# An attention and expert kernel: early Q/K parts moved to ScalarE and GpSimd, five banks in the last unit, routing reordered

## The chip, the cores and the metric

One core of one Trainium2 chip runs the whole program. The metric is device time in microseconds; the kernel before took 1055.47 us (median of 3 runs, 1055.44 to 1056.58). Engines are named as in the profile: PE (TensorE, with its weight loads as PEld), DVE (VectorE), ACT (ScalarE), POOL (GpSimd), SP (SyncE, which issues most DMAs).

## The reference, cut to what matters

Cross-attention of 4 batches of 512 image tokens on 1601 context rows (16 heads of 16), with a small MLP behind it, and then a layer with one shared expert and 8 routed experts of which each token takes two.

```python
def _L0_xattn_ref(x, y, Wq, bq, Wk, bk, Wv, bv, W1, b1, W2, b2):
    q = (x @ Wq + bq).reshape(B, N, NUM_HEADS, HEAD_DIM)
    k = (y @ Wk + bk).reshape(B, M, NUM_HEADS, HEAD_DIM)
    v = (y @ Wv + bv).reshape(B, M, NUM_HEADS, HEAD_DIM)
    scores = jnp.einsum('bnhd,bmhd->bhnm', q, k) * scale
    attn = jax.nn.softmax(scores, axis=-1)
    out = jnp.einsum('bhnm,bmhd->bnhd', attn, v).reshape(B, N, IMAGE_DIM)
    h = jax.nn.relu(out @ W1 + b1)
    return h @ W2 + b2
...
probs = jax.nn.sigmoid(logits)
scores, idx = jax.lax.top_k(probs, TOP_K)
cw = (jax.nn.one_hot(idx, E_ROUTED, dtype=x.dtype) * scores[..., None]).sum(-2)
out = shared
for e in range(E_ROUTED):
    out = out + cw[..., e:e + 1] * _expert(x, Wg[e], Wu[e], Wd[e])
...
x = x + jnp.tanh(g_xattn[0]) * _L0_xattn_ref(_layernorm(x, axis=-1), ctx_768, ...)
x = x + jnp.tanh(g_ffn[0]) * _L0_ffn_ref(_layernorm(x, axis=-1), ...)
```

## The kernel before, in words

Attention runs in 16 units: 4 batches times 4 groups of four heads. Q and K of a batch are made in two halves of 128 rows (dt 0 and 1): 2 jobs ("Q", b, dt) and 8 jobs ("K", b, dt, q), each a product in a bank of `ring_ps`. ACT adds the bias and writes the value rounded to fp32r, the high part (L643, L648); DVE subtracts that from the product again and so writes the low part (L1017, L1024). SP then copies high and low rows into the stacks `kst` and `qst` of a unit by DMA (L448, L452, L467, L469): a unit multiplies stacks of high and low rows.

Every unit has two passes over its scores. First the maxima: 26 "pairs" ("S", u, ...) are two matmuls of 512 keys into one of two slots of `gu_ps` (L839), each reduced by DVE (L985, or L987 for the last 68 keys, 1.2 us and 0.7 us); then ("MX", u) turns the 16 maxima (L779), DVE negates them into `mneg` (L1032), and SP writes them as one more row of `qst` (L474). Second the values: 13 steps of four transposed score tiles `st` (L852, one for each head, in banks of `ring_ps`), four exponentials on ACT (L690), and four products with V into `pv_ps` (`pv`, L867). Between the tiles of a step stand the other jobs: the pairs of the next unit, V, the sums ("SUM"), the MLP of the batch before, and in the last unit the transposes and logits of the second layer ("XT2", "LT", "LG").

Four things set the order. `schedule()` writes it out by hand: `first` and `early` before the first step, then for each step a `chunk` of pairs and a list of jobs; unit 1's first six pairs stand ahead of the first step, the other 20 go into unit 0's steps. `ring` gives each user of `ring_ps` a bank in turn, three banks in all, and PE waits until the user three places before has been emptied (`free_bank`). `probs` has two buffers: the first exponential of a step waits until the `pv` two steps back is done. And each engine has one queue in program order.

The second layer (`experts`) runs as 16 shared tiles and 39 blocks of routed tokens on one pipeline, i = 0 to 56: in step i PE makes gate and up of tile i (`gate_up`, L1359), turns the hidden tile i-1 (`turn_hidden`, L1368) and multiplies tile i-2 down (`down`, L1379), which DVE takes out (`take_y`, L1556 or L1561). The first 10 shared tiles cover the routing. In step 2 DVE does `route()` (L1445 to L1462) from the logits, for which ACT does one exponential (L1268) and loads its table; in step 3 PE counts (`ranks`) and DVE computes slots; in steps 4 and 5 DVE and ACT build one-hot rows (`make_hot`, `make_rows`); in step 6 PE inverts them (`inverse`, L1316) and DVE makes the lists (`make_lists`). DVE also splits the experts' weights into high and low parts in these steps (`rest_gate` L1542, `rest_up` L1547, 16 calls), and the first routed block waits for all of them. Weights arrive by DMA meanwhile.

Of the kernel before, what the change touches and what calls it, by code (L numbers as in the profile page):

```python
# [62 lines left out]
AT_REST = {5: range(0, 3), 6: range(3, 8)}  # L63
# [4 lines left out]
LEAD = 3  # L68
NR = 3
NSP = 2  # L70
# [43 lines left out]
def schedule():  # L114
# [61 lines left out]
    parts = [k[6:7], k[7:8], q[1:2]] + [[("V", 0, g, i)] for g in range(VJOBS) for i in range(min(2, MT - 2 * g))]  # L176
# [5 lines left out]
    for n, pair in enumerate(ahead):  # L182
        early += [pair] + (parts.pop(0) if parts else [])
    b = B - 1
# [114 lines left out]
def attention(nc, I, x1, stats, mv, veps, power, rstd, tg, ident, rows_dram,  # L299
# [11 lines left out]

    ring = list(before)
    for u, mt, _, jobs in steps:
        m = MT * u + mt
        mids, tops = [job for job in jobs if job[0] != "MX"], [job for job in jobs if job[0] == "MX"]
        ring += [("st", idx) for idx in (4 * m - 1, 4 * m) if idx >= 0] + mids
        ring += [("st", 4 * m + 1), ("st", 4 * m + 2)] + tops
    ring += [("st", 4 * MT * UNITS - 1)] + last_jobs
    ring_at = {user: n for n, user in enumerate(ring)}

    def bank(user):

        return ring_at[user] % NR

    def bank_owner(user):

        n = ring_at[user]
        return ring[n - NR] if n >= NR else None

    by_act = [job for job in order if job[0] in ("XT", "V", "OT", "W1")]  # L330
    by_dve = [job for job in order if job[0] not in ("XT", "V", "OT", "W1")]
# [8 lines left out]
    with ExitStack() as ctx:  # L340
# [10 lines left out]


# [44 lines left out]
        hi_ready = sem("hi_ready")  # L397
        xn_ready = sem("xn_ready")
# [23 lines left out]
        def _(sp):  # L422
# [19 lines left out]
            def load_first_stacks():  # L442
# [3 lines left out]
                sp.wait_ge(free_dve, freed["K", 0, 0, 1])  # L446
                for c, part in ((0, 0), (1, 1), (2, 0)):
                    sp.dma_start(kst[0][c:P:4, :, half].bitcast(F32), kc[0:64, 0, part, half].bitcast(F32)  # L448
                                 ).then_inc(half_loaded, 16)
                sp.wait_ge(free_dve, freed["Q", 0, 0])  # L450
                for c, part in ((0, 0), (1, 0), (2, 1)):
# [1203 lines left out]
```

## Time and profile before

| | |
|---|---|
| median of 3 runs | 1055.47 us |
| the profiled execution's own time | 1053.79 us |
| its span, first to last instruction | 1052.0 us |
| mean granted PE clock | 0.995 |
| PE / DVE / ACT / POOL busy | 1020.6 / 675.8 / 610.3 / 204.0 us |
| start to the first step of unit 0 | 0 to 63.8 us |
| units 0 to 14, steps | 63.8 to 684 us |
| last unit, steps | 684 to 728 us |
| end of attention and MLP | 728 to 749 us |
| shared tiles with the routing | 749 to 810 us |
| routed blocks and the end | 810 to 1052 us |

A busy PE is not PE at its peak, because matmuls overlap and their ends are modelled; where PE waits is read from the timeline and the chain of waits. The span's own start is 0 in all times below.

### The profile page before, as it was taken

The page shows a single profiled execution, that of the slowest core. Times are in us where ns is not written, and L with a number is a line of the kernel's source. Part 1 is how long each engine was busy: PE and PEld are TensorE (multiplying, and loading weights), DVE is VectorE, ACT ScalarE, POOL GpSimd, SP SyncE. Part 2 cuts the span into 40 slices and gives each one's busy share as a digit, 9 for nine tenths or more (in the row PEclk, how much of TensorE's full clock was granted, in tenths as well). Part 3 has the DMA queues.
Part 4 walks back from the last instruction along what each step waited for, and adds up shares of the span by engine and source line. Part 5 has one row for each costly group of instructions (what it writes and reads, how often), then busy time and mean ns, then how long its engine had stood idle before and what let it go on. Part 6 is the DMA issues. An engine that isn't in the chain of part 4 may idle for free. (4 is left out here: it accounts for less than half of the span.)

```text
span 1052.0 us, 15631 instructions
## 1 busy us (share of the span) xinstructions
PE 1020.6 (97%) x5729; PEld 548.4 (52%) x5729; DVE 675.8 (64%) x920; ACT 610.3 (58%) x1139; POOL 204.0 (19%) x212
## 2 busy tenths in 40 slices
PE   5889999999999999999999999999989999999998
PEld 3443445343545434444444353333656888888865
DVE  4989787896677798578788678621388333222226
ACT  2148777887577777577787667774356222222221
POOL 5018400008200003600000031020003233333310
PEclk9989999999999999999999999999999999999999
DMA  8361130430303313113033020110491011111207
GB/s 199 88 165 26 38 64 1 126 63 1 62 2 62 91 36 62 41 23 63 1 63 63 1 62 2 36 55 32 159 342 31 31 51 51 50 52 55 50 26 239
DMA packets 38281, 70.15 MB, mean 67 GB/s; under 512 B 6848, under 2 KB 23360, under 8 KB 38208
## 3 DMA queue, kind: packets, MB, share of 16 engines
q1 hardware_dynamic: 33072, 57.88, 21.2%
q0 software_dynamic: 3744, 10.23, 3.2%
q10 hardware_dynamic: 1392, 1.05, 0.4%
q8 instruction: 48, 0.79, 0.3%
q14 instruction: 25, 0.20, 0.1%
HBM read 33.70 MB, written 9.31 MB: 41 GB/s over the span
## 5 line engine op out<-in xcount | busy, mean ns | idle before, releaser
L690 ACT ACTIVATE probs<-ring_ps 128x512 f32<-128x512 f32 (+1 forms) x832 | 441.6, 598 | 136.3 <-PE ring_ps L852 132.9
L985 DVE TENSOR_REDUCE mpart<-gu_ps 128x2 f32<-128x1024 f32 x384 | 457.0, 1221 | 82.6 <-PE gu_ps L839 82.6
L852 PE MATMUL ring_ps<-qst,kst 64*128 64x512 f32 (+1 forms) x832 | 232.1, 464 | 3.7 <-ACT probs L690 3.1
L867 PE MATMUL pv_ps<-probs,vp 128*32 128x512 f32 (+2 forms) x1664 | 222.1, 606 | 0.7 <-ACT probs L690 0.7
L852 PEld LDWEIGHTS ring_ps<-qst,kst 64*128 64x128 f32 (+1 forms) x832 | 100.9, 181 | 218.6 <-ACT probs L690 125.1
L839 PE MATMUL gu_ps<-kst,qst 63*128 63x512 f32 (+1 forms) x1024 | 178.4, 397 | 8.4 <-DVE mpart L985 7.0
L839 PEld LDWEIGHTS gu_ps<-kst,qst 63*128 63x128 f32 x1024 | 92.2, 186 | 68.4 <-DVE mpart L985 43.5
L1205 ACT ACTIVATE h_sb<-gu_ps 128x512 f32<-128x512 f32 x55 | 32.8, 596 | 135.8 <-PE gu_ps L1359 135.7
L1412 DVE TENSOR_TENSOR h_sb<-h_sb,gu_ps 128x512 f32<-128x512 f32 x55 | 37.8, 687 | 112.6 <-ACT h_sb L1205 112.1
L294 POOL TENSOR_SCALAR veps<-mv 128x4 f32<-128x4 f32 x8 | 1.9, 232 | 533.8 <-DVE mv L954 283.6
L1379 PE MATMUL y_ps<-wd,hT 128*128 x312 | 73.8, 379 | 0.0
L1196 POOL DMA_INDIRECT picked<-ysb,target x39 | 38.5, 988 | 131.7 <-DVE ysb L1561 131.7
L867 PEld LDWEIGHTS pv_ps<-probs,vp 128*32 128x32 f32 (+2 forms) x1664 | 32.4, 107 | 57.3 <-issue 42.9
L1359 PE MATMUL gu_ps<-wgu_lo,xb_hi 128*128 x156 | 61.2, 392 | 0.0
L1379 PEld LDWEIGHTS y_ps<-wd,hT 128*128 128x128 f32 x312 | 56.2, 190 | 6.0
L1359 PE MATMUL gu_ps<-cold,parts 128*128 128x512 f32 x118 | 53.6, 595 | 0.3 <-PEq L340 0.3
L1183 POOL DMA_INDIRECT xb<-rows,token x39 | 40.7, 1044 | 60.8 <-DVE token L1517 39.0
L1211 ACT ACTIVATE xb_hi<-t_ps 128x256 fp32r<-128x256 f32 x39 | 15.0, 385 | 49.3 <-PE t_ps L1325 49.3
L1561 DVE COPY ysb<-y_ps 128x256 f32<-128x256 f32 x39 | 16.6, 425 | 33.1 <-PE y_ps L1379 33.1
L662 ACT ACTIVATE vp<-ring_ps 128x512 f32<-128x512 f32 (+1 forms) x28 | 15.9, 568 | 34.1 <-PE ring_ps L727 34.1
L1246 ACT ACTIVATE hT<-ht_ps 128x512 f32<-128x512 f32 x55 | 32.5, 592 | 3.6 <-PE ht_ps L1368 3.6
L1024 DVE SCALAR_TENSOR_TENSOR parts<-ring_ps,bk,parts 128x402 fp32r<-128x402 f32 (+1 forms) x32 | 20.3, 635 | 22.2 <-ACT parts L648 22.1
(205 smaller groups left out, 1146.6 us busy)
## 6 DMA issues: line engine op xcount, KB each, us to landing
kst<-parts SPq DMA_DIRECT2D x45, 401.0 KB, 5.3
qst<-parts SPq DMA_DIRECT2D x48, 128.0 KB, 4.5
wgu<-in_WgT SPq DMA_DIRECT2D x16, 256.0 KB, 8.5
wgu<-in_WuT SPq DMA_DIRECT2D x16, 256.0 KB, 8.6
wd<-in_WdT SPq DMA_DIRECT2D x8, 512.0 KB, 9.7
wgu<-picked SPq DMA_DIRECT2D x8, 512.0 KB, 8.5
cold<-in_ctxT SPq DMA_DIRECT2D x3, 800.5 KB, 4.1
cold<-in_ctxT SPq DMA_DIRECT2D x6, 400.2 KB, 5.9
```

The lines of the kernel that those rows point to most:

```text
L690: nc.scalar.activation(probs[0:w, m % NPB, h, :], ring_ps[0:w, bank(("st", idx)), :], ACT.Exp, scale=SCALE).then_inc(exp_done, 1)
L839: last = nc.tensor.matmul(out, qst[u % NKB][rows, p, i * P:(i + 1) * P], kst[u % NKB][rows, p, keys], start=True, stop=True)
L852: nc.tensor.matmul(ring_ps[0:w, bank(("st", idx)), :], kst[u % NKB][rows, h // 2, mt * P:mt * P + w], qst[u % NKB][rows, h // 2, :], start ...
L867: last = nc.tensor.matmul(pv_ps[32 * h:32 * h + c1 - c0, :], values[:, c0:c1], probs[0:w, m % NPB, h, :], start=(mt == 0), stop=(mt == MT ...
L985: nc.vector.tensor_reduce(mpart[:, :, p, t, q], s_ps[:, n % NSP], AX.X, ALU.max).then_inc(s_free, 1)
L1183: pool.indirect_dma_start(xb[:, r % NXB, :], None, rows_dram[:], bass.IndirectOffsetOnAxis(ap=token[:, r:r + 1], axis=0)).then_inc(xb_load ...
L1196: pool.indirect_dma_start(picked_dram[:], bass.IndirectOffsetOnAxis(ap=target[:, r:r + 1], axis=0), ysb[:, r % NXB, :], None).then_inc(y_s ...
L1205: nc.scalar.activation(h_sb[:, i % 2, :], gu_ps[:, i % 2, 0, :], ACT.Silu).then_inc(silu_done, 1)
L1246: nc.scalar.activation(hT[:, i % 2].rearrange("p k n -> p (k n)"), ht_ps[:, i % 2, :], ACT.Copy).then_inc(ht_copied, 1)
L1359: last = nc.tensor.matmul(gu_ps[:, i % 2, f, :], x, w, start=(n == 0 and not begun), stop=(n == len(products) - 1))
L1379: last = nc.tensor.matmul(y_of(i), hT[:, i % 2, k, :], w, start=(k == 0), stop=(k == FK - 1))
L1412: nc.vector.tensor_tensor(h_sb[:, i % 2, :], h_sb[:, i % 2, :], gu_ps[:, i % 2, 1, :], ALU.mult).then_inc(h_ready, 1)
```

## The change

Five things are changed.

1. Start. PE does 48 transposes of the identity before its first real product. The stack copies of the first unit are issued as soon as the part that each needs is written, the high parts before the low ones. The second half (dt 1) of batch 0's Q and K is emptied by ACT alone: a second activation writes the unrounded value, and POOL subtracts the high part in place.
2. Unit 0. Of unit 1's pairs two stand ahead of the first step and 24 go into the ten steps up to its maxima, so three in some steps; the last V job goes into step 0.
3. Last unit. Ring users take five banks in turn, the two further ones in `gu_ps`, whose slot 1 no pair needs any more; the tiles of each step run two tiles further ahead, and all jobs stand behind the four tiles and ahead of `pv`.
4. The wait for all pairs ahead of the shared tiles goes; a wait for all exponentials stands ahead of the last product of the attention part.
5. Routing. ACT's exponential comes ahead of the copy of tile 1's hidden rows; DVE takes out tile 0 inside `route()`, behind the maxima; the first three `rest_gate` move from step 5 into step 6, ahead of the lists.

PE, start of the program; `L770` and `L822` are K, `L748` and `L800` the transposes of x, `L755` and `L807` Q, `L839` and `L891` the pairs, before:

```order
L770 MATMUL ring_ps<-cold,w_kv 128x402 x2
L748 MATMUL ring_ps<-ident,xn 128x128 x8
L770 MATMUL ring_ps<-cold,w_kv 128x402 x2
L755 MATMUL ring_ps<-xnT,wq 128x512 x2
L770 MATMUL ring_ps<-cold,w_kv 128x400 x4
L770 MATMUL ring_ps<-cold,w_kv 128x402 x4
L839 MATMUL gu_ps<-kst,qst 128x512 x4
```

and now:

```order
L927 MATMUL ring_ps<-ident 128x128 x48
L822 MATMUL ring_ps<-cold,w_kv 128x402 x2
L800 MATMUL ring_ps<-ident,xn 128x128 x8
L822 MATMUL ring_ps<-cold,w_kv 128x402 x2
L807 MATMUL ring_ps<-xnT,wq 128x512 x2
L822 MATMUL ring_ps<-cold,w_kv 128x400 x4
L822 MATMUL ring_ps<-cold,w_kv 128x402 x4
L891 MATMUL gu_ps<-kst,qst 128x512 x4
```

Only the 48 transposes are new there; the order behind them stands.

PE in two steps of the last unit (`L852`, `L906` the tiles; `L867`, `L921` pv; `L795`, `L847` XT2; `L801`, `L853` LT), before:

```order
L852 MATMUL ring_ps<-qst0,kst0 128x512 x2
L795 MATMUL ring_ps<-ident,parts 128x128 x4
L852 MATMUL ring_ps<-qst0,kst0 128x512 x2
L867 MATMUL pv_ps<-probs,vp 32x512 x3
L867 MATMUL pv_ps<-probs,vp 17x512
L852 MATMUL ring_ps<-qst0,kst0 128x512 x2
L801 MATMUL ring_ps<-parts,wr 8x512 x2
L852 MATMUL ring_ps<-qst0,kst0 128x512 x2
L867 MATMUL pv_ps<-probs,vp 32x512 x3
L867 MATMUL pv_ps<-probs,vp 17x512
```

and now, where `gu_ps` rows are those in the two further banks:

```order
L906 MATMUL gu_ps<-qst0,kst0 128x512
L906 MATMUL ring_ps<-qst0,kst0 128x512 x3
L847 MATMUL gu_ps<-ident,parts 128x128 x4
L921 MATMUL pv_ps<-probs,vp 32x512 x3
L921 MATMUL pv_ps<-probs,vp 17x512
L906 MATMUL gu_ps<-qst0,kst0 128x512
L906 MATMUL ring_ps<-qst0,kst0 128x512 x3
L853 MATMUL gu_ps<-parts,wr 8x512 x2
L921 MATMUL pv_ps<-probs,vp 32x512 x3
L921 MATMUL pv_ps<-probs,vp 17x512
```

The job has moved from between the tiles to behind them, next to `pv`.

DVE in the routing (`L1556`, `L1504` take_y; `L1412`, `L1468` the hidden tile), before:

```order
L1452 MAX top<-prob 128x8 x16
L1455 MAX_INDEX top_i<-top,prob 128x8 x16
L1457 CAST top_f<-top_i 128x128
L1459 TENSOR_TENSOR hot<-count_f,top_f 128x128 x2
L1462 TENSOR_TENSOR cnt<-hot 128x128
L1556 SCALAR_TENSOR_TENSOR x<-y_ps,tg,x 128x256
L1412 TENSOR_TENSOR h_sb<-h_sb,gu_ps 128x512
```

and now:

```order
L1521 MAX top<-prob 128x8 x16
L1504 SCALAR_TENSOR_TENSOR x<-y_ps,tg,x 128x256
L1525 MAX_INDEX top_i<-top,prob 128x8 x16
L1527 CAST top_f<-top_i 128x128
L1529 TENSOR_TENSOR hot<-count_f,top_f 128x128 x2
L1532 TENSOR_TENSOR cnt<-hot 128x128
L1468 TENSOR_TENSOR h_sb<-h_sb,gu_ps 128x512
```

Tile 0 is taken out four rows of DVE work earlier, and the counts are written one row of work later.

The diff, cut to its core:

```diff
-AT_REST = {5: range(0, 3), 6: range(3, 8)}
+AT_REST = {6: range(3, 8)}
+BEGUN = 2
+WARM = 48
 NR = 3
+NX = 2
...
         for n, chunk in enumerate(scores(u)):
             at = start + n * MT // len(scores(u))
+            if u == 1:
+                at = (n - BEGUN) * (MT - LEAD) // (len(scores(u)) - BEGUN)
...
+    others[0].append(("V", 0, VJOBS - 1))
...
+    def ahead_of_values(u, job):
+        return job[0] == "MX" or u == UNITS - 1
+
+    def tiles_of(m):
+        first, last = (2 if m > MT * (UNITS - 1) else 0), (2 if m >= MT * (UNITS - 1) else 0)
+        return list(range(max(4 * m - 1 + first, 0), min(4 * m + 3 + last, 4 * MT * UNITS)))
...
+    widened = ring_at["st", 4 * MT * (UNITS - 1)]
+    narrowed = ring_at[last_jobs[0]]
+    for n, user in enumerate(ring):
+        count_of = NR + NX if widened <= n < narrowed else NR
+        turn = (turn + 1) % count_of if n else 0
+        banks[user], owners[user] = turn, held.get(turn)
+        held[turn] = user
...
+    by_pool = [job for job in order if job[0] in ("Q", "K") and job[1:3] == (0, 1)]
+    by_act = [job for job in order if job[0] in ("XT", "V", "OT", "W1") or job in by_pool]
...
-                sp.wait_ge(free_dve, freed["K", 0, 0, 1])
-                for c, part in ((0, 0), (1, 1), (2, 0)):
...
+                for part, copies, done, at in ((0, (0, 2), hi_ready, hi_count["K", 0, 0, 1]),
+                                               (1, (1,), free_dve, freed["K", 0, 0, 1])):
+                    sp.wait_ge(done, at)
+                    for c in copies:
+                        sp.dma_start(kst[0][c:P:4, :, half].bitcast(F32), kc[0:64, 0, part, half].bitcast(F32)
+                                     ).then_inc(half_loaded, 16)
...
+                if b == 0 and hg // 2 == 1:
+                    sp.wait_ge(low_ready, len(by_pool))
...
+            for job in by_pool:
+                dt, cols = job[2], slice(KCUT[job[3]], KCUT[job[3] + 1]) if job[0] == "K" else slice(0, N)
+                part = kc if job[0] == "K" else qc
+                pool.wait_ge(free_act, freed[job])
+                nc.gpsimd.tensor_tensor(part[:, dt, 1, cols], part[:, dt, 1, cols].bitcast(F32),
+                                        part[:, dt, 0, cols].bitcast(F32), ALU.subtract).then_inc(low_ready, 1)
...
+                    if job in by_pool:
+                        nc.scalar.activation(qc[:, dt, 1, :].bitcast(F32), slot, ACT.Identity, bias=bq[:, dt:dt + 1]
+                                             ).then_inc(free_act, 1)
...
             pe.wait_ge(pool_ready, 2)
+            for n in range(WARM):
+                nc.tensor.transpose(ring_ps[:, 0, 0:P], ident[:], ident[:])
...
-            pe.wait_ge(free_act, freed["V", 0, VJOBS - 1])
...
-            pe.wait_ge(s_free, len(pairs))
...
+            pe.wait_ge(exp_done, 4 * MT * UNITS)
             begin_shared(1, 0, 0)
...
                 if i < JOBS:
                     silu(i)
+                if i == AT_LOGITS:
+                    act.wait_ge(logits_ready, 1)
+                    nc.scalar.activation(prob[:], logit[:], ACT.Exp, scale=-1.0).then_inc(exp_ready, 1)
                 if i >= 1:
                     take_ht(i - 1)
...
                 for t in range(TT):
                     last = nc.vector.max(top[:, t, :], prob[:, t, :])
                 own(last)
+                take_y(0)
...
                 if i == AT_INVERSE:
+                    for e in range(3):
+                        rest_gate(e)
                     make_lists()
...
-                if i >= 2:
+                if i > 2:
                     take_y(i - 2)
```

## Rows read from the trace of the kernel before

**Rows 1.** The page, busy time and share of the span.

```profile
PE 1020.6 (97%) x5729; PEld 548.4 (52%) x5729; DVE 675.8 (64%) x920; ACT 610.3 (58%) x1139; POOL 204.0 (19%) x212
```

**Rows 2.** The chain that ended last, routing: start us, us, what.

```profile
759.76 1.28 ACT L1268
...
767.17 0.49 DVE x L1556
767.80 1.97 PE y_ps L1379 x8
...
781.93 3.40 DVE wgu_lo L1542 x3
...
787.45 2.12 PE t_ps L1316 x16
789.57 3.25 PE y_ps L1379 x8
...
811.72 1.62 PE gu_ps L1359 x6
```

**Rows 3.** Timeline of PE, the start: start us, us, operation, count.

```profile
9.56 3.02 PE L770 MATMUL ring_ps<-cold,w_kv 128*128 128x402 f32 x4 [9.56 <-DMA w_kv<-in_Wk]
12.37 1.91 PE L748 MATMUL ring_ps<-ident,xn 128*128 128x128 f32 x8
14.08 2.04 PE L770 MATMUL ring_ps<-cold,w_kv 128*128 128x402 f32 x4
...
17.67 5.55 PE L770 MATMUL ring_ps<-cold,w_kv 128*128 128x400 f32 x16
24.57 0.74 PE L839 MATMUL gu_ps<-kst,qst 63*128 63x512 f32 x4 [1.35 <-DMA qst<-parts]
```

**Rows 4.** Stretches of the start: busy us (count), granted clock, DMA share, GB/s.

```profile
14.00:16.00 2.00, 2.00 (x7) 1.15 (x6) 0.02 (x1) 0.67 (x2) 2.00 (x2) 1.00 0.81 285
...
22.00:24.00 2.00, 1.22 (x4) 0.38 (x2) 0.68 (x2) 1.10 (x2) 0.00 (x0) 1.00 1.00 192
```

**Rows 5.** DVE's groups by shape, 25.1 to 56.9 us.

```profile
L985 DVE TENSOR_REDUCE mpart<-gu_ps 128x2 f32<-128x1024 f32 x24 | 27.7, 1218 | 0.8 <-PE gu_ps L839 0.8
L1024 DVE SCALAR_TENSOR_TENSOR parts<-ring_ps,bk,parts 128x400 fp32r<-128x400 f32 x2 | 1.3, 630 | 0.1
L1017 DVE SCALAR_TENSOR_TENSOR parts<-ring_ps,bq,parts 128x512 fp32r<-128x512 f32 x1 | 0.8, 750 | 0.5 <-ACT parts L643 0.5
```

**Rows 6.** Timeline, from unit 0's maxima to its tenth step.

```profile
56.64 0.22 DVE L993 TENSOR_REDUCE mx<-mpart 128x16 f32<-128x64 f32 x1
...
57.62 0.62 SPq L474 DMA_DIRECT2D qst<-mneg  x1
...
63.81 0.39 PE L852 MATMUL ring_ps<-qst,kst 64*128 64x512 f32 x1
...
89.84 0.50 PE L852 MATMUL ring_ps<-qst,kst 64*128 64x512 f32 x2
...
92.44 0.50 PE L852 MATMUL ring_ps<-qst,kst 64*128 64x512 f32 x2
```

**Rows 7.** Stretches with the maxima's row, and with the clock's fall.

```profile
60.00:61.00 1.00, 1.00 (x6) 0.50 (x5) 0.74 (x2) 0.60 (x1) 0.00 (x0) 1.00 0.00 0
...
66.20:73.00 6.80, 6.54 (x28) 2.87 (x24) 4.99 (x6) 4.19 (x8) 0.00 (x0) 0.50 1.09 279
```

**Rows 8.** Timeline of PE in the last unit, `pv` of single steps.

```profile
691.84 1.06 PE L867 MATMUL pv_ps<-probs,vp 128*32 128x512 f32 x8
...
694.43 1.06 PE L867 MATMUL pv_ps<-probs,vp 128*32 128x512 f32 x8
...
697.52 1.06 PE L867 MATMUL pv_ps<-probs,vp 128*32 128x512 f32 x8
```

**Rows 9.** Groups by shape in the last unit, 686 to 728.5 us, ACT's largest.

```profile
L690 ACT ACTIVATE probs<-ring_ps 128x512 f32<-128x512 f32 x48 | 25.8, 596 | 10.6 <-PE ring_ps L852 10.1
```

**Rows 10.** One stretch in the routing, with the clock's fall.

```profile
790.00:791.00 1.00, 1.00 (x4) 0.77 (x3) 0.90 (x5) 1.00 (x2) 0.00 (x0) 0.50 0.00 0
```

More of the change, by code:

```diff
@@ L175, in schedule @@
     early = []
-    parts = [k[6:7], k[7:8], q[1:2]] + [[("V", 0, g, i)] for g in range(VJOBS) for i in range(min(2, MT - 2 * g))]
+    parts = [k[6:7], k[7:8], q[1:2]] + [[("V", 0, g, i)] for g in range(VJOBS - 1) for i in range(2)]
     for n, pair in enumerate(scores(0)):
@@ L181, in schedule @@
     early += [("MX", 0)]
-    for n, pair in enumerate(ahead):
+    for pair in ahead:
         early += [pair] + (parts.pop(0) if parts else [])
+    for part in parts:
+        early += part
     b = B - 1
@@ L635, in take @@
                 kind, b = job[0], job[1]
-                slot = ring_ps[:, bank(job)]
+                slot = bank_of(job)
                 if kind == "Q":
@@ L649, in take @@
                                          bias=bk[:, dt:dt + 1]).then_inc(hi_ready, 1)
+                    if job in by_pool:
+                        cols = slice(KCUT[q], KCUT[q + 1])
+                        nc.scalar.activation(kc[:, dt, 1, cols].bitcast(F32), slot[:, 0:KCUT[q + 1] - KCUT[q]],
+                                             ACT.Identity, bias=bk[:, dt:dt + 1]).then_inc(free_act, 1)
                 elif kind == "XT":
@@ L740, in do @@
             def do(job):
-                slot = ring_ps[:, bank(job)]
+                slot = bank_of(job)
                 free_bank(bank_owner(job))
@@ L890, in _ @@
                 for job in jobs:
-                    if job[0] != "MX":
+                    if not ahead_of_values(u, job):
                         do(job)
@@ L894, in _ @@
                     score(pair)
-                st(at + 1)
-                st(at + 2)
+                for idx in tiles_of(m)[lead:]:
+                    st(idx)
+                for pair in chunk[2:]:
+                    score(pair)
                 for job in jobs:
-                    if job[0] == "MX":
+                    if ahead_of_values(u, job):
                         do(job)
-                if at > 0:
-                    pv(MT * u + mt - 1)
-            st(4 * MT * UNITS - 1)
+                if m > 0:
+                    pv(m - 1)
             pv(MT * UNITS - 1)
@@ L995, in do @@
             def do(job):
-                slot = ring_ps[:, bank(job)]
+                slot = bank_of(job)
                 kind = job[0]
-                if kind in ("XT", "V", "OT", "W1"):
+                if job in by_act:
                     return
@@ L1064, in _ @@
                         do(job)
-                for pair in chunk[1:2]:
+                for pair in chunk[1:]:
                     top_of(pair)
@@ L1440, in take_last, with take_y @@
                                       ).then_inc(xn2T_ready, 1)
+            def take_y(i):
+                dve.wait_ge(y_full, i + 1)
+                r, t = i - EARLY, tile_of(i)
+                if t is not None:
+                    if t >= EARLY and i + 2 > combined_at(t):
+                        dve.wait_ge(combined, t + 1)
+                    nc.vector.scalar_tensor_tensor(out=x1[:, t, :], in0=y_of(i), scalar=tg[:, 1:2],
+                                                   in1=x1[:, t, :], op0=ALU.mult, op1=ALU.add).then_inc(y_out, 1)
+                    return
+                if r >= NXB:
+                    dve.wait_ge(y_stored[r % NXB], 16 * (r // NXB))
+                nc.vector.tensor_copy(ysb[:, r % NXB, :], y_ps[:, 0:D]).then_inc(y_out, 1)
             def route():
```

79 lines of the change are left out of this document (35 added, 44 removed).

## The prediction, made before the changed kernel ran

> **What bounds the kernel now.** I read the page's busy shares first, then the chain of waits, then the timeline of those stretches in which PE waits. PE is busy 97% of the span [rows 1], so what counts is where PE waits or runs slowly. The routed blocks behind 810 us have no such place. The steps of units 0 to 14 have hardly any: a plain step lasts 92.44 - 89.84 = 2.60 us [rows 6] and is full of PE's work. Three stretches are left, and the change touches each: the start up to 63.8 us, the last unit, and the routing.
>
> At the start PE's first products run at half pace: the four records of the first K job take 3.02 us, 0.67 us apart, while the sixteen behind 17.67 take 5.55 us, 0.34 apart [rows 3]. That is 1.2 GHz and then 2.4 GHz, though the clock column reads 1.00 there. Then PE waits 1.35 us for the stack copies (first pair at 24.57, [rows 3]), and from there DVE sets the pace up to the maxima at 56.64 us: 24 reduces of 1.18 us from start to start, two short ones, and three low parts, with hardly an idle moment [rows 5, 6]. In the last unit ACT waits 10.1 us for tiles [rows 9], and a step lasts 694.43 - 691.84 = 2.59 us without a job and 3.09 us with a transpose job [rows 8]. In the routing the chain leaves PE for ACT and DVE twice: at 759.76 (table load, exponential, top two, then tile 0's take-out at 767.17, for which `down(1)` waits 3.1 us), and at 781.93 (three weight splits, 3.40 us, ahead of the one-hot rows) [rows 2].
>
> **Start, S.** If the 48 transposes raise the clock, the first product still starts at about 9.56, when its weights land. (A transpose at half pace is 1.91 / 8 = 0.24 us at most [rows 3], 0.21 from start to start, and half of that at full pace; begun at 1.7 us when the identity is ready, 48 take 10.2 us at half pace and 5.1 at full, so a rise by about 8 us lets them end at 9.5.) Then K takes 1.35 us, not 2.8, the transposes of x 0.85, not 1.7, and the second K 1.35. Q, which gave way to the next K job at 17.67, now does so at 14.8, begun at 13.1; the four K jobs behind it take 5.4 us and end at 20.2.
>
> The stack copies can't gain as much. Q is written by 16.3 (ACT, then DVE 0.75 [rows 5]) and its copies are issued by about 17.6, but the DMA engines are still at the weights until 16 us (285 GB/s in 14 to 16), and move stacks at 192 GB/s [rows 4]. The first half's six copies are 64 rows each, three of 804 numbers and three of 512: 987 KB, which take 5.1 us: the first pair starts at 21.1, 3.5 us earlier. POOL's five subtractions and ACT's five further activations (about 3 us) lie in time in which both idle.
>
> From first reduce to maxima it took 31.5 us. Three low parts go, 2 x 0.63 + 0.75 = 2.0 us [rows 5]. PE is late next: a K job of 1.35 us or Q of 1.7 us between pairs makes DVE wait about 0.25 and 0.4 us. So 1.35 us are gained, and the maxima are ready at 51.8, 4.85 us earlier.
>
> Then only two pairs and two V halves stand ahead of the first tile, 3.3 us, against six pairs: from 52.2 to 55.8. The row of maxima isn't late: before, its copy was issued at 57.62 and the DMA engines were idle by 60 [rows 6, 7], so it takes 2.4 us at most and is there at 55.3. The first tile moves from 63.81 to 55.8, 8.0 us.
>
> Part is given back. Ten steps now hold 24 pairs: DVE needs 22 x 1.175 + 2 x 0.72 for them and 2.1 us for statistics, 29.4 us, and with a wait at the entry and 0.25 us in some two-pair steps about 30.4. Before, the same ten steps took 92.44 - 63.81 = 28.6 us, 26.0 of it at 2.60 us for each and the rest lost to a clock of 0.50 for 6.8 us [rows 6, 7]. PE's own work in them is 26.0 + 4 x 0.43 + 0.5 = 28.2 us, below DVE's. So **S = -8.0 + 1.9 = -6.1 us**. Bounds: the clock may fall again in these steps (+2.5 us, as it cost before), or the copies may land with the old delay behind their issue, an issue 4 us earlier (-7.0 in all): -3.6 to -7.0 us while the clock does rise at the start.
>
> **Units 0 to 14 behind that.** The order is unchanged, so 0; the V job moved into step 0 is in the sum above. The second half's stacks now wait for POOL, in SP's queue ahead of the maxima's copy of unit 1: POOL is free from 19 us and needs about 1.1 us for each of five parts, done by 36, and the copies are due at 64.
>
> **Last unit, L.** No row shows five banks, so I follow the loop. A step's first exponential needs `pv` of two steps back. Without a job the fourth tile of a step now waits for the exponential of the tile five places before, and `pv` ends (0.05 + 0.43 + 1.06) before ACT has done its other three exponentials at 0.515 each: ACT sets the pace, 2.1 us, against 2.59. With a transpose job the loop is 0.05 + 0.43 (tile) + 0.43 (job) + 1.06 (`pv`, [rows 8]) + 0.06 + 0.55 = 2.6 us against 3.09 [rows 8]. With LT (1.7 us on PE) it is 3.9 against 3.66, a loss, since the job now stands straight ahead of `pv`. Summed: one plain step 0.5, the first 0.1, SUM and four XT2 steps 5 x 0.48 = 2.4, two LT steps -0.5, two LG steps 0.3 each, and the end, where two waits of ACT's go, 1.3: **L = -4.4 us**. From below, all 52 exponentials and the copy at 0.52 us are 27.6 us of the 42.3 between 686.1 and 728.4, but PE's own work is 33, so at most -8.5; from above, if the loop with a job gains nothing, -1.9.
>
> **Routing, R.** On ACT the table load stands ahead of the wait for the logits; with the copy of tile 1 gone from before it, it runs at 757.6 to 758.9, and the exponential at 758.9, 2.15 us earlier than now (759.76 + 1.28 + 0.02 [rows 2]). If the load waits too, 0.85. The counts come at 767.15 - 2.15 + 0.48 = 765.5. `down(1)` needs tile 0 taken out, now at 762.2, and follows the hidden tile at 764.6 without its wait of 3.1 us, ends at 766.4, and `ranks` follow, at 766.9 in all against 770.0: -3.1. Next, DVE: one-hot rows without the 3.40 us of splits are ready by 782.2, PE gets to the inverse at 781.9, and its 32 matmuls at 0.113 us end at 785.6, against 789.57 [rows 2]: -3.95. What is late next is DVE: from 789.6 to 810.9 it was busy without a break until the last weight split, for which the first routed block waits; that stretch of 21.3 us moves to 785.75 and ends at 807.0, while PE would be there at 806.0 with the clock kept, or 807.8 with the fall to 0.50 [rows 10] that follows the inverse. Before, PE was there at 811.7 [rows 2]. So **R = -4.3 us**, -3.3 to -4.7. The weights' DMA ends before 787 (the traffic falls to nothing there), when ACT needs the fifth expert at 785.7 and the last at 788.6.
>
> **Sum.** S + L + R = -6.1 - 4.4 - 4.3 = -14.8 us. The profiled execution took 1053.79 us, 1.8 more than its span of 1052.0, and becomes 1039.0; it is 1.7 below the median shown, so the forecast for the median is 1055.47 - 14.8 = **1040.7 us**.
>
> **Rivals.** *The transposes don't raise the clock.* Then they hold PE until 11.9, the first product starts 2.3 us later and still slowly, Q ends about 1.5 us later than now, and only the earlier issue (0.8 us) and the later terms are left: S is -6.1 + 4.3 = -1.8, total -10.5, 1045.0 us. For it: the clock column says nothing here. Against it: the clock rose at about 14.9, out of a stretch from 11.7 of which 1.7 us, half, was transposes [rows 3]; when PE had only pairs with waits between them, as before 66.2 us, it fell. The Trainium skill says in "TensorE: Matmul & The Clock Gate", Part 4: PE-mode transpose, that the full clock doesn't engage for transposes since they don't count as busy work in the same way; by that rule this rival holds. The stretch ahead of the rise speaks against it, but doesn't settle it.
>
> *The clock falls in the fuller steps.* PE waits for DVE in three-pair steps as it did ahead of 66.2; S loses 2.5 us, total -12.3, 1043.2 us. For it: same pairs, same waits [rows 7]. Against: `pv` and tiles fill the gaps now.
>
> *Slower.* Units 1 to 14 are 182 steps that keep a rhythm between three banks, two `probs` buffers and two pair slots. If they are entered with DVE behind and settle 0.1 us above 2.60, 18 us are lost and the kernel takes 1058.9; it decides from 14.8 / 182 = 0.08 us a step. For it: the entry is new. Against it: right after the disturbed stretch that ends at 73 us the steps were back at 2.60 [rows 6].
>
> **How the numbers follow.** Forecast 0.60, no rise 0.20, fall in the steps 0.15, slower 0.05. The range for 8 in 10 takes in the first three: from 1040.7 less a share of L's and S's bounds (-4.7) to the no-rise case with a microsecond over it, 1036.0 to 1046.0; the forecast's own is 1037 to 1043.5. A measurement here can't tell less than 0.2%, 2.1 us, from no change. Faster: the first three, 0.95, and hardly any of the last: 0.95. Same: 0.01. Slower: 0.04.
>
> **What will show it.** Right: the first K records 0.34 us apart and Q begun before 14 us; first pair at about 21; the first tile at 56 and the tenth step at 86; 2.1 us and 2.6 us from `pv` to `pv` in the last unit, and 3.9 with LT; no wait ahead of `down(1)`; the first routed block's up products 4 to 4.6 us earlier from the start of the second layer. Wrong: K records 0.67 us apart behind the transposes; a clock of 0.50 between 50 and 85 us; steps above 2.65 us in units 1 to 14; `pv` still 3.1 us apart with a job.

## The result, and the profile after

The changed kernel takes 1041.7 us (median of 4 executions, 1039.91 to 1041.95); the kernel before, run beside it, 1055.9 (1055.44 to 1056.58). The ratio is 0.9861, 95% interval 0.9844 to 0.9878: faster by 14.2 us, or 1.4%. The forecast was 1040.7. The two profiled executions differ by less, 1053.79 - 1041.95 = 11.8 us, since that of before was 2.1 us under its median. The page's first row answers to [rows 1]:

```profile
PE 1021.9 (98%) x5777; PEld 555.7 (53%) x5777; DVE 672.5 (65%) x915; ACT 610.9 (59%) x1144; POOL 208.5 (20%) x217
```

PE's busy time looks like that of before, with 48 instructions more. But those 48 transposes hold PE for 8.1 us (1.62 to 9.73) in which it only waited before. Without them its busy time is 6.8 us shorter, in part because work that had run at half pace no longer does, and the other 5.3 of the 12.1 us that the span lost were idle time. The start, timeline of PE, against [rows 3]:

```profile
9.57 1.52 PE L822 MATMUL ring_ps<-cold,w_kv 128*128 128x402 f32 x4
10.92 1.04 PE L800 MATMUL ring_ps<-ident,xn 128*128 128x128 f32 x8
12.58 1.62 PE L822 MATMUL ring_ps<-cold,w_kv 128*128 128x402 f32 x4 [0.62 <-DVE parts L1080]
14.03 1.88 PE L807 MATMUL ring_ps<-xnT,wq 128*128 128x512 f32 x4
15.75 5.55 PE L822 MATMUL ring_ps<-cold,w_kv 128*128 128x400 f32 x16
21.95 0.74 PE L891 MATMUL gu_ps<-kst,qst 63*128 63x512 f32 x4 [0.66 <-DMA qst<-parts]
```

The first K job is at full pace: nothing but transposes ran ahead of it. The eight transposes of x are at full pace too (1.04 us, 1.91 before). The second K job waits 0.62 us for a bank. The first pair starts 2.6 us earlier than before. The marks behind it, timeline (unit 0's maxima, first tile, tenth step), against [rows 6]:

```profile
52.30 0.22 DVE L1049 TENSOR_REDUCE mx<-mpart 128x16 f32<-128x64 f32 x1
...
55.84 0.50 PE L906 MATMUL ring_ps<-qst,kst 64*128 64x512 f32 x1
...
85.72 0.50 PE L906 MATMUL ring_ps<-qst,kst 64*128 64x512 f32 x2
```

The tenth step begins 92.44 - 85.72 = 6.7 us earlier. And where before had a clock of 0.50 for 6.8 us [rows 7], the stretches of the changed kernel (busy us, granted clock third from the end) have none:

```profile
58.00:68.00 10.00, 8.66 (x56) 3.17 (x52) 9.92 (x11) 7.01 (x15) 2.54 (x4) 1.00 0.94 254
68.00:86.00 18.00, 16.93 (x118) 7.07 (x116) 17.37 (x22) 13.09 (x25) 10.07 (x12) 1.00 0.37 100
```

The last unit, timeline of PE, against [rows 8]: a plain step takes 2.27 us (684.74), one with a transpose job 2.43 (687.01) or 2.86 (689.44). From unit 14's last `pv` to the end it takes 39.35 us, 42.34 before.

```profile
684.74 1.06 PE L921 MATMUL pv_ps<-probs,vp 128*32 128x512 f32 x8
...
687.01 1.06 PE L921 MATMUL pv_ps<-probs,vp 128*32 128x512 f32 x8
...
689.44 1.06 PE L921 MATMUL pv_ps<-probs,vp 128*32 128x512 f32 x8
690.43 0.50 PE L906 MATMUL gu_ps<-qst,kst 64*128 64x512 f32 x1
690.44 1.35 PE L906 MATMUL ring_ps<-qst,kst 64*128 64x512 f32 x3
691.72 0.66 PE L847 MATMUL gu_ps<-ident,parts 128*128 128x128 f32 x4
692.30 1.06 PE L921 MATMUL pv_ps<-probs,vp 128*32 128x512 f32 x8
```

The routing, chain of waits, against [rows 2]; it lies on PE throughout now, and `down(1)` (755.40) waits for nothing:

```profile
755.40 1.73 PE y_ps L1435 x8
757.13 0.22 PE t_ps L1360 x2
...
772.64 4.31 PE t_ps L1372 x32
776.95 3.59 PE y_ps L1435 x8
780.54 4.18 PE gu_ps L1415 x8
...
798.53 1.62 PE gu_ps L1415 x7
```

The ranks come 3.3 us sooner after the second layer's start, but the first routed block only 2.5 us: the clock fell at the inverse as it had before [rows 10], and for longer (6.8 us at half pace, 3.4 before). Stretch 774 to 782, mean clock 0.57:

```profile
774.00:782.00 8.00, 8.00 (x31) 6.30 (x31) 6.34 (x17) 3.90 (x4) 2.42 (x3) 0.57 0.51 173
```

Three of the four executions had a mean clock of 0.997 and took 1041.67 to 1041.95 us; one had 1.000 and took 1039.91.

### The profile page after: what moved, and what is told of

Its sections match the earlier page's. It is cut to its first block and busy times, and to the rows that moved or that the text cites. A ratio compares the mean times of both kernels' runs of the same rounds, so it can differ in the third digit from the quotient of the medians.

```text
span 1039.9 us, 15726 instructions
## 1 busy us (share of the span) xinstructions
PE 1021.9 (98%) x5777; PEld 555.7 (53%) x5777; DVE 672.5 (65%) x915; ACT 610.9 (59%) x1144; POOL 208.5 (20%) x217
## 5 line engine op out<-in xcount | busy, mean ns | idle before, releaser
L743 ACT ACTIVATE probs<-ring_ps 128x512 f32<-128x512 f32 x816 | 433.1, 598 | 125.5 <-PE ring_ps L906 118.4
L906 PE MATMUL ring_ps<-qst,kst 64*128 64x512 f32 x816 | 224.8, 461 | 2.8 <-ACT probs L743 2.1
L921 PE MATMUL pv_ps<-probs,vp 128*32 128x512 f32 (+2 forms) x1664 | 222.7, 604 | 0.6 <-ACT osb L677 0.6
L906 PEld LDWEIGHTS ring_ps<-qst,kst 64*128 64x128 f32 x816 | 98.5, 180 | 207.6 <-ACT probs L743 117.8
L891 PE MATMUL gu_ps<-kst,qst 63*128 63x512 f32 (+1 forms) x1024 | 178.4, 396 | 6.6 <-DVE mpart L1041 5.4
L891 PEld LDWEIGHTS gu_ps<-kst,qst 63*128 63x128 f32 x1024 | 91.9, 186 | 66.7 <-DVE mpart L1041 42.3
L1468 DVE TENSOR_TENSOR h_sb<-h_sb,gu_ps 128x512 f32<-128x512 f32 x55 | 37.8, 687 | 113.3 <-ACT h_sb L1261 112.8
L921 PEld LDWEIGHTS pv_ps<-probs,vp 128*32 128x32 f32 (+2 forms) x1664 | 33.1, 107 | 57.2 <-issue 41.3
L1415 PEld LDWEIGHTS gu_ps<-cold,parts 128*128 128x128 f32 x118 | 22.5, 194 | 22.8 <-issue 22.1
L1424 PEld LDWEIGHTS ht_ps<-ident,h_sb 128*128 128x128 f32 x220 | 27.4, 141 | 13.2 <-issue 6.8
```

The costliest lines, as they stand in the source:

```text
L743: nc.scalar.activation(probs[0:w, m % NPB, h, :], bank_of(("st", idx))[0:w], ACT.Exp, scale=SCALE).then_inc(exp_done, 1)
L891: last = nc.tensor.matmul(out, qst[u % NKB][rows, p, i * P:(i + 1) * P], kst[u % NKB][rows, p, keys], start=True, stop=True)
L906: nc.tensor.matmul(bank_of(("st", idx))[0:w], kst[u % NKB][rows, h // 2, mt * P:mt * P + w], qst[u % NKB][rows, h // 2, :], start=True, st ...
L921: last = nc.tensor.matmul(pv_ps[32 * h:32 * h + c1 - c0, :], values[:, c0:c1], probs[0:w, m % NPB, h, :], start=(mt == 0), stop=(mt == MT ...
L1415: last = nc.tensor.matmul(gu_ps[:, i % 2, f, :], x, w, start=(n == 0 and not begun), stop=(n == len(products) - 1))
L1424: last = nc.tensor.transpose(ht_ps[:, i % 2, k * P:(k + 1) * P], h_sb[:, i % 2, k * P:(k + 1) * P], ident[:])
```

## Experiments

Medians of 4 to 6 executions; ratios stand against the kernel before, run beside it. The changed kernel's is 0.9861 (0.9844 to 0.9878). An interval is about 2 us to either side, so the time alone doesn't tell no_warm, low_on_dve, both pairs_ahead, start_five and both mixed kernels from the changed kernel. What is said of them rests mainly on one trace each. Where executions differ, those whose mean clock was 1.000 are compared as well; the changed kernel has one such, 1039.91 us.

**Start: no_warm.** `WARM = 48` becomes 0.

> The changed kernel without the 48 transposes at its start. Theory A, that they alone raised TensorE's clock before the first product of K (four instructions 1.52 us where before took 3.02; the eight transposes of x 1.04 where before took 1.91): the first pair of the scores begins near 24.4 us instead of 21.95, nothing behind it gives this back, 1044.2 (+2.5). Rival B, that the first pair's time came from the loads that are issued once the high parts are written: first pair near 22 us, 1041.7 to 1042.2. Rival C, that the sum of the prediction was right (3.5 us of the start and more): 1045.2 or above.

1043.5 us (1042.03 to 1045.28), ratio 0.9875 (0.9854 to 0.9896). Timeline of PE, and the maxima:

```profile
10.10 3.02 PE L822 MATMUL ring_ps<-cold,w_kv 128*128 128x402 f32 x4 [10.10 <-DMA w_kv<-in_Wk]
...
24.16 0.73 PE L891 MATMUL gu_ps<-kst,qst 63*128 63x512 f32 x4 [0.57 <-DMA qst<-parts]
...
54.49 0.22 DVE L1049 TENSOR_REDUCE mx<-mpart 128x16 f32<-128x64 f32 x1
```

Half pace is back. From first product to first pair it is 14.06 us, against 12.38 with the transposes and 15.01 before: the transposes give 1.7 us, the earlier loads 0.95. From the pair on everything is only shifted (30.33 and 30.35 us to the maxima). A. Of the 2.2 us by which the first pair is later than in the changed kernel, 0.5 are the weights, which landed later here, so the transposes' own share is smaller than the 2.5 expected.

**Start: low_on_dve.** `by_pool = [job for job in order if False]`, so VectorE makes all low parts.

> The changed kernel with the low parts of all of batch 0's Q and K made by VectorE from PSUM, as in the kernel before (ScalarE's second copy and Pool's subtraction are gone). Theory A, that VectorE alone set the stretch from the first maximum (22.5) to unit 0's last (52.3, 29.8 us, 31.8 in the kernel before): five low parts of some 0.65 us come back, of which 2.0 to 3.3 us show: first tile at 58 to 59 us instead of 55.84, 1043.7 to 1045.0. Rival B, that TensorE's pairs set that stretch: first tile unchanged, 1041.7. Rival C, that ScalarE and Pool were slower than VectorE would have been (Pool's subtraction of 512 columns is longer than VectorE's), so that undoing it wins: below 1041.3.

1043.0 us (1041.84 to 1044.05), ratio 0.9871 (0.9850 to 0.9891). From first pair to maxima 33.03 us against 30.35, and the first tile at 58.95: A, with the time at its lower end. But 1.0 us of the 2.7 is probably not VectorE's own: PE waited 0.86 and 0.55 us for reduces, the clock fell to a mean of 0.61 between 36 and 40 us, and before took 32.07 without a fall. By that the part is worth 1.7 us, and the median says 1.3.

**Start: pairs_ahead and pairs_ahead_kept.** First unit 1's pairs back to their old places:

```
-            if u == 1:
+            if False:
                 at = (n - BEGUN) * ...
```

> The changed kernel with unit 1's pairs of score tiles placed as before: six of them ahead of the first tile instead of two, the rest one every step or so. Theory A (from the traces): between unit 0's maxima and the first tile 3.6 us come back, and the ten steps give 1.3 us of it: 1044.0 (+2.3), first tile at 59.5 us. Theory B (the prediction's own terms, 3.15 and 1.9): 1043.0 (+1.3). Rival C, that VectorE has the same maxima to take in either place and the end of unit 0 doesn't move: 1041.7, unit 0's tenth step at 85.7 us as now.

1042.4 us (1041.37 to 1044.81), ratio 0.9866 (0.9845 to 0.9886): 0.7 us by the median, where A said 2.3, B 1.3 and C nothing. In the trace the first tile is at 59.58, as A says, and the tenth step at 89.89, not at C's 85.7; but this execution is the longest of the six. Its stretches:

```profile
56.00:60.00 4.00, 2.37 (x11) 0.85 (x9) 3.73 (x4) 0.69 (x2) 2.76 (x4) 0.95 0.00 0
60.00:68.20 8.20, 7.75 (x27) 3.26 (x26) 5.81 (x6) 4.15 (x8) 0.96 (x2) 0.50 0.49 148
```

PE is busy 2.37 of 4 us while the last pairs ahead wait for VectorE, and then runs at 0.50 for 8 us, as in [rows 7]. Its mean clock was 0.993; four of the other executions had 0.997, the changed kernel's usual figure, and took 1041.4 to 1042.8. So it seems that the old places cost time only when the clock falls; none of those four was traced. The second kernel fills that gap:

```
+            free_bank(bank_owner(("st", 0)))
+            for n in range(24):
+                nc.tensor.transpose(bank_of(("st", 0))[:, 0:P], ident[:], ident[:])
             pe.wait_ge(free_dve, freed["MX", 0])
```

> As pairs_ahead (six of unit 1's pairs ahead of the first tile), with 24 transposes of the identity in the time in which TensorE waits for unit 0's maxima, some 2.7 us of work that nothing reads. In pairs_ahead the clock was 0.50 from 59.6 to 68.1 us and the kernel before had it at 0.50 in the same steps; the changed kernel kept 1.00. Theory A, that what the move of the pairs bought in the traces (2.4 us) is this fall and not fewer maxima ahead of the tiles: clock 1.00 from 56 to 76, the ten steps 27.0 to 27.5 us instead of 30.4, unit 1's maxima at 86.5 at the latest instead of 89.98, time 1041.7 +- 0.4, no worse than the changed kernel. Rival B, that the steps are short of work whatever the clock is: ten steps 28.5 us or more, 1043.5. Rival C, that the transposes don't hold the clock: as pairs_ahead, 1042.4 to 1044.8.

1043.4 us (1043.16 to 1044.0), ratio 0.9884 (0.9867 to 0.9902). PE's timeline, unit 1's maxima, and a stretch:

```profile
59.59 2.84 PE L939 MATMUL ring_ps<-ident 128*128 128x128 f32 x24
62.36 0.49 PE L906 MATMUL ring_ps<-qst,kst 64*128 64x512 f32 x1
...
88.75 0.22 DVE L1052 TENSOR_REDUCE mx<-mpart 128x16 f32<-128x64 f32 x1
...
60.00:68.20 8.20, 7.82 (x54) 4.67 (x52) 5.77 (x6) 4.02 (x8) 0.88 (x2) 1.00 0.38 114
```

The transposes kept the clock, and the ten steps take 26.3 us (the tenth begins at 88.66), 4.0 less than in pairs_ahead. But they started behind the last pair and not in the gap, and held back the first tile by 2.8 us, so A's time is missed and the time is B's. From maxima (52.62) to maxima it is 36.1 us, 33.4 without the filler's 2.8: as good as the changed kernel's 33.5. By this subtraction, what the move of the pairs buys is the clock, not fewer reduces; no trace shows the old places at full clock without a filler.

**Start: start_five.** The first five jobs get five banks (`FIVE = 5`); the second pair waits for those it takes over.

```
-        count_of = NR + NX if widened <= n < narrowed else NR
+        count_of = NR + NX if widened <= n < narrowed or n < FIVE else NR
```

> The changed kernel; its first five jobs (K, two XT, K, Q) get five banks instead of three in turn, two of them lent by the pairs' tile, so that the second product of K does not wait for VectorE's low part of the first (0.62 us at 12.58, which the prediction had not foreseen). Theory A: second K at 11.96, Q at 13.4, first pair at 21.3 instead of 21.95, all behind it as much earlier: 1041.1 (-0.6). Rival B, that the loads of the stacks wait for VectorE's low parts and not for TensorE: first pair stays at 21.9, 1041.7. Rival C, that the first pair is now bound by the transfers' own 2 us and the issue on SP's queue, of which half moves: 1041.4.

1040.7 us (1039.42 to 1044.1), ratio 0.9852 (0.9830 to 0.9875). From first product to first pair 11.67 us against 12.38: A, 0.7 us. In the profiled execution unit 0's first steps lost 1.5 us again (35.0 us from maxima to maxima, 33.5 in the changed kernel):

```profile
60.00:62.00 2.00, 2.00 (x12) 0.20 (x8) 2.00 (x3) 1.09 (x2) 0.00 (x0) 0.50 1.03 254
```

Even with the pairs moved, then, the clock can fall there.

**Last unit: last_old and last_mid.** last_old has NX = 0, the old tiles of a step and jobs between them. last_mid changes one line of the changed kernel:

```
-        return job[0] == "MX" or u == UNITS - 1
+        return job[0] == "MX"
```

> The changed kernel with the last unit as in the kernel before: three banks, a tile carried over each step, jobs between the tiles. Theory A, that the part is worth what the stretch lost in the traces, 42.3 - 39.35 = 3.0 us: 1044.7. Rival B, that it is worth the 4.4 us of the prediction and another place hides 1.4 of them: 1046.1. Rival C, that the last unit gains from the earlier parts and not from its banks: 1042.5 or less. The stretch from unit 14's last value products to the end of the last unit takes 42.3 us by A and B, under 40.5 by C.

> The changed kernel, but in the last unit the jobs stand between its two pairs of tiles again (five banks stay). Theory A, that the fourth tile of a step with a job waits for a bank whose exponential waits for the value products two steps back (4 tiles take 1.28 us there where 4 x 0.215 = 0.86 are their work, 0.43 too much): behind the job the wait is covered. Steps with a transposing job 2.86 -> 2.43 us (4 of them), the two pairs of steps with the logits' products 7.16 -> 6.36 us: last unit 39.35 -> about 36.4 us, time 1038.8 (1041.7 - 2.9). Rival B, that the place of the job is nothing to these steps (TensorE or the exponentials fill them either way): 39.3 us and 1041.7. Rival C, that a job between the tiles holds back two tiles until VectorE has emptied its bank, and ScalarE with them: slower, about 0.1 us a job, 1042.6.

last_old: 1045.6 us (1042.90 to 1046.0), ratio 0.9897 (0.9874 to 0.9921), 3.9 us, between A and B. The trace of this kernel has 42.9 us for the stretch, near A's and B's 42.3, and a fall of the clock at its end, where PE had waited 0.86 us for VectorE and 0.31 us for ScalarE ahead of the last `pv`:

```profile
719.00:721.00 2.00, 1.69 (x13) 0.34 (x16) 0.00 (x0) 1.53 (x3) 0.00 (x0) 0.89 0.00 0
721.00:723.00 2.00, 2.00 (x9) 0.50 (x2) 0.00 (x0) 0.42 (x1) 0.00 (x0) 0.50 0.00 0
```

Four of the five executions had a mean clock of 0.995. The fifth had 1.000 and took 1042.90: 3.0 us above the changed kernel's 1039.91. So the part itself is worth A's 3.0 us, and what the median has on top goes with the clock.

last_mid: 1037.0 us (1036.87 to 1039.08), ratio 0.9826 (0.9803 to 0.9848), 4.7 below the changed kernel. Its steps with transposes take 2.44 us:

```profile
690.30 1.06 PE L921 MATMUL pv_ps<-probs,vp 128*32 128x512 f32 x8
691.29 0.50 PE L906 MATMUL gu_ps<-qst,kst 64*128 64x512 f32 x1
691.29 0.50 PE L906 MATMUL ring_ps<-qst,kst 64*128 64x512 f32 x1
691.73 0.66 PE L847 MATMUL ring_ps<-ident,parts 128*128 128x128 f32 x4
692.31 0.49 PE L906 MATMUL ring_ps<-qst,kst 64*128 64x512 f32 x1
692.31 0.50 PE L906 MATMUL gu_ps<-qst,kst 64*128 64x512 f32 x1
692.74 1.06 PE L921 MATMUL pv_ps<-probs,vp 128*32 128x512 f32 x8
```

Behind the job no tile waits: while PE transposes, ScalarE does the exponential that frees the bank. The mechanism of A holds. The stretch becomes 37.65 us, 1.7 shorter and not 2.9; 0.95 of what is missing is a fall of the clock at its start (mean 0.57 from 682.07 to 686.07), where two steps took 5.65 us, 4.70 in the changed kernel. The rest of this execution's gain lies in the routing, where its fall was shorter (the products behind the inverse 3.39 and 3.55 us against 3.59 and 4.18, the inverse 3.48 against 4.31). Where both kernels kept the clock, 1036.9 stands against 1039.9, the 2.9 of A; the 4.7 between the medians sets an execution without a fall against one with a fall.

**Routing: route_old.** The four edits of the routing undone.

> The changed kernel with the routing's four edits undone (the result of down(0) taken after the routing's arithmetic, the exponential behind the copy of the transposed hidden rows, three splits back in step 5). Theory A (from the two traces: the ranks are done 3.3 us sooner after the second layer's start, 2.5 us of it reach the first routed block): 1044.2 (+2.5), and down(1) waits about 3 us for VectorE again. Theory B (the prediction's own term): 1046.0 (+4.3). Rival C, that VectorE's splits behind the lists are the bound whatever the routing does, so that the routing's 3.3 us are lost before the first block: 1041.7.

1045.9 us (1043.81 to 1048.62), ratio 0.9906 (0.9888 to 0.9924): 4.2 us, by its size the prediction's term (B). Stretches and `down(1)`:

```profile
754.00:758.00 4.00, 1.20 (x6) 0.50 (x4) 3.86 (x42) 3.02 (x5) 0.00 (x0) 1.00 1.07 379
758.00:760.00 2.00, 1.72 (x4) 1.48 (x5) 0.73 (x2) 1.01 (x1) 0.00 (x0) 0.51 1.06 367
...
758.28 3.52 PE y_ps L1435 x8
```

PE waits again, and here the clock falls right behind the wait: `down(1)` takes 3.52 us, 1.97 in [rows 2]. The wait alone is 3.1 us, as before; that 1.6 comes on top is a matter of the execution. Without it the trace has the first routed block about 2.5 us later than the changed kernel's, which is A. So B's number is met with a fall in it that B does not have, and the trace alone would leave A.

**Routing: mixed_inverse and mixed_rest.** One product of `down(4)` behind each eight of the inverse's; in mixed_rest also `rest_gate(3)` ahead of the lists.

```
+                    if n % HOT == HOT - 1:
+                        down(AT_INVERSE - 2, n // HOT)
```

> The changed kernel; in the second layer the four products of down(4) (128x256, 0.43 us each) are put one behind each eight of the 32 products with 40 columns, in place of behind all of them. The clock was 0.50 from about 775 to 782 us there, and the products after it took 3.59 and 4.18 us where 1.73 and 3.43 are usual (2.6 us). Theory A, that 4.3 us of nothing but 40-column products let the clock fall, and that VectorE, not TensorE, then ends last before the first routed block (its splits end 798.25, TensorE's first half 798.53 to 799.9): the clock stays 1.00, but the lists begin 3 x 0.43 = 1.3 us later and so do VectorE's splits; second half of the block at about 799.6: 1041.4. Rival B, that TensorE alone is the bound: 1039.1. Rival C, that the clock falls all the same: 1041.7 to 1043, with 0.50 in the records around 777.

> As mixed_inverse, and the fourth split of the gate weights (1.15 us a piece) is done by VectorE ahead of the lists instead of behind them, in the time in which it waits for the inverse (1.2 us before, 2.5 by mixed_inverse). Theory A (clock kept, VectorE the bound): its splits end about 0.15 us later than in the changed kernel, 798.4, and the second half of the first block begins there and not at 799.9: 1040.2 (-1.5), 1.2 us less than mixed_inverse. Rival B (TensorE the bound): the same time as mixed_inverse. Rival C (the clock falls all the same): 1041.7 or more.

mixed_inverse: 1041.7 us (1041.54 to 1042.57), ratio 0.9868. mixed_rest: 1040.7 us (1039.94 to 1041.61), ratio 0.9859. A both times by the median, for mixed_inverse with 0.3 us more. The mean clock was 1.000 in four of five and three of five executions. Stretch of mixed_rest, and the end of mixed_inverse's chain:

```profile
772.00:778.00 6.00, 6.00 (x46) 5.56 (x44) 5.38 (x9) 2.01 (x4) 0.00 (x0) 1.00 0.96 329
```

```profile
797.39 1.59 PE gu_ps L1418 x6
798.98 0.62 issue
799.60 1.64 PE gu_ps L1418 x6
```

PE is ready at 798.98 and waits 0.62 us. VectorE's last split ends at 798.79, and the second half starts 0.81 us behind it, as in mixed_rest (797.27 and 798.08); PE's queue reads a register between the two. With the clock kept, then, VectorE is the bound, and its lists, which start later by the three products now ahead of them (1.3 us), eat what the clock gives. mixed_inverse's executions with a clock of 1.000 took 1041.5 to 1041.8 us, above the changed kernel's 1039.91: the mixing spares the fall and costs time where there is none.

**All at once: combined and with_pool.** combined is last_mid, mixed_rest and start_five; with_pool also gives two splits to Pool.

> The changed kernel with what the earlier runs point to, all at once: jobs between the tiles in the last unit (last_mid), down(4) among the 40-column products with the fourth gate split ahead of the lists (mixed_rest), five banks for the first jobs (start_five). Theory A, that they add up, the clock's part counted once: 1036.9 (last_mid where it kept the clock) - 0.65 = 1036.2, with little scatter between executions. Rival B, that mixed_rest costs 0.5 us where the clock would have held anyway: 1036.7. Rival C, that the earlier start leaves TensorE idle longer before unit 0's first steps, so that the clock falls there as in start_five (1.5 us): 1037.7.

> As combined, and Pool makes the splits of the first two experts' up weights (128x1024 a piece), which VectorE made. Theory A, that VectorE is what the first routed block waits for since the clock is kept (in mixed_rest 0.49 us before the hidden rows' transposes and 0.62 us before the block's second half): VectorE has 2.4 us less, both waits go, 1035.1 (combined - 1.1). Rival B, that Pool's work on the same memory slows VectorE's splits (1.15 us each) or comes late itself: the same as combined or worse. Rival C, that the bound is elsewhere (ScalarE's high parts, the gathered rows): the same as combined.

combined: 1037.6 us (1036.01 to 1039.80), ratio 0.9831 (0.9813 to 0.9849), the same as last_mid within what can be measured. The two executions with a clock of 1.000 took 1036.0 and 1036.6, which is A; the median is C's, and the slowest had 0.995, but no trace shows where its clock fell. with_pool: 1039.1 us (1038.84 to 1039.46), ratio 0.9844 (0.9829 to 0.9859), slower than combined by 1.4, and by 2.2 to 3.0 where both kept the clock. Timelines of POOL and DVE:

```profile
787.52 4.66 POOL L1256 TENSOR_TENSOR wgu_lo<-wgu,up_hi 128x1024 fp32r<-128x1024 f32 x2
...
787.59 5.69 DVE L1635 TENSOR_TENSOR wgu_lo<-wgu,up_hi 128x1024 fp32r<-128x1024 f32 x1
```

Rival B, and far worse than its words: one split, 1.15 us otherwise, took 5.69 us of VectorE while Pool made its two. It ended 1.1 us behind Pool's second, as if it had hardly run until then. The transposes of the second block waited 2.48 us for what stood behind it.

## Why the prediction was right, and where its terms were off

**The transposes and the clock.** Right: they raised it, by themselves, and the rival fell. So did the rule of the Trainium skill ("TensorE: Matmul & The Clock Gate", Part 4: PE-mode transpose) that it had stood on; this case's rows, 1.52 against 3.02 us, decide against it, and the transposes took the full pace themselves (1.04 against 1.91 us for eight). The trace names no mode of the product, so that these ran in the mode that the page means is taken from the kernel's call, `nc.tensor.transpose`.

The working for them was off by a little: with 10.2 us at half pace and a rise by 8 us the 48 would have ended at 9.95 and not at 9.5. They ended at 9.57, with no wait behind them, so the rise came at about 7.3 by the same sum. In pairs_ahead and mixed_rest they took 7.1 us, and PE then waited 1.2 and 0.7 us for its first product.

**First pair.** Predicted 21.1, came at 21.95: the gain of 3.5 us was 2.6. The step that failed is "the second K 1.35" right behind the transposes of x. Three banks were counted as free; the fourth user needs the bank of the first K job, whose low part VectorE ends at 12.5. That wait is 0.6 us, and start_five took it away: 0.7 of the 0.85 us that were missing.

**Maxima to first tile.** Predicted 51.8 and 55.8, measured 52.3 and 55.84. VectorE's relief was 1.7 us, not 1.35, and the shorter stretch behind the maxima 3.6, not 3.2: three errors that cancel.

**The ten steps.** Predicted 30.4, measured 29.9; S is -6.7 against -6.1. But its account of why was incomplete. It booked the move of the pairs as 3.2 us won and 1.9 given back. Measured against steps that keep the clock (26.3 us), the move wins 3.6 and gives back 3.6, so it wins nothing of its own; what it buys is that the clock no longer falls. The prediction took the fall of before as a fixed 2.6 us in its ten steps and as a risk of the new order, not as a cost that some executions of the old order pay and others may not.

**Units 0 to 14.** Predicted 0, measured +0.4 (6.7 to 6.3 us). The slower rival didn't occur.

**Last unit.** Predicted -4.4, -3.0 by the traces, -3.0 again where last_old kept the clock, -3.9 by its median. Three terms were mis-sized. The largest is the steps with LT and LG: each pair takes 7.16 us, 6.84 before, where 6.8 were counted, 0.7 us in all. The loop of a step with a transpose job was given as 2.6 us: it is 0.21 from `pv` to the exponential, 0.60 for it, 0.05 and 0.43 for the tile, 0.58 for the job (0.43 assumed), 0.99 for `pv`, in all 2.86. Three steps took that, 0.8 us too much, and two took 2.43, which gave 0.4 back. And the plain step takes 2.27 us, not 2.1. (The outer bound of -8.5 took PE's own work as 33 us, from which -9.3 follows; in the changed kernel PE was busy for 36.2 us of the stretch.) The prediction described the chain rightly and didn't see that the place of the job makes it.

**Routing.** Ranks -3.1 predicted, -3.3 measured: right. The block's start was to be 4.3 us earlier and was 2.5 by the traces, under the bound of 3.3. The step that failed is the fall behind the inverse, booked with the 1.8 us that it had cost before: the inverse took 4.31 us and not 3.6, and the products behind it 2.6 us more than at full clock, 3.3 in all, with VectorE's chain starting 0.6 later. So PE came last, and not DVE. DVE as what is late next holds where the clock is kept, shown by mixed_inverse. Undone, the part is worth 4.2 by the median, near the 4.3, but 1.6 us of that are a fall behind `down(1)` in the trace, and 2.5 are left.

**Sum.** -14.8 predicted, -14.2 between medians, -11.8 between the profiled executions. The last is what the sum was worked out for, since it starts from the same profiled execution of before. Its parts are -6.7, +0.4, -3.0 and -2.5, and the end of attention (part 4 of the change) gives nothing, 20.9 us either way. So the mechanisms were right and two sizes, those of the last unit and the routing, too large by 3.2 us together; that the medians come within 1 us of the forecast is in part luck. By the medians the parts undone one by one give 1.8 + 1.3 + 0.7 + 3.9 + 4.2 = 11.9 us; the earlier loads (0.95 in the trace) were not undone, and 1.3 us stay open, of the size of the scatter. These parts hold falls of the clock themselves, so that they add up is no proof. The likeliest account is that before pays falls of the clock in more places (its executions had mean clocks of 0.989 to 0.995); that was not shown by a run of its own.

## What to carry to other kernels

Behind a wait of PE's, or a row of narrow products, look at the granted clock and price the fall with the wait: it came back as 1 to 4 us behind several different idle stretches here, and not in every execution. Where two engines free each other's buffers in a loop, put independent work between the request and the next one, not behind both: with the clock kept, that one line was worth as much as the two extra banks with all that came with them, 3.0 us each. And before moving work from VectorE to Pool, ask what VectorE runs at that moment.

## What the runs showed of the hardware

- 48 fp32 transposes of 128x128 raised TensorE's clock: the next 402-column products went from 3.02 to 1.52 us for four.
- At or behind 32 products of 40 columns in a row it fell to 0.50 though PE was busy without a break, in six of the eight profiled executions with such a row (not in low_on_dve and pairs_ahead_kept). With one 256-column product behind each eight it stayed at 1.00 in all four that were profiled, and the mean was 1.000 in seven of ten executions of the two mixed kernels.
- The same wait of 3.1 us ahead of `down(1)` was followed by a granted clock of 0.51 in route_old, where the products took 3.52 us, and by hardly any loss before (1.97 us).
- A VectorE subtraction of 128x1024, fp32 in SBUF, took 5.69 us beside two of Pool's in the same memory (2.35 us each), 1.22 us alone. At the start, where VectorE read PSUM for its reduces, Pool's subtractions beside them cost it next to nothing: a reduce took 1219 ns (1227 at most) between 22 and 33 us, 1215 ns in low_on_dve, where Pool makes none.
- The first product began between 9.3 and 10.1 us after the start in the profiled executions, and the first pair moved with it; differences below that between two traces need a common mark, as used above.
